# Attention on one core: query products in the scores' third PSUM bank, and the upper value products in tiles 4, 5, 8, 9 instead of 8 to 11

## The chip, the core and the metric

The kernel runs on one core of a Trainium2 chip. The metric is the device time of one execution in microseconds (us), lower is better. The core has four compute engines that each run their own instruction stream in order and meet at semaphores: TensorE (PE, matrix products), VectorE (DVE), ScalarE (ACT) and GpSimd (POOL); SyncE (SP) issues the DMAs. PE writes its products into PSUM, which has 8 banks of 128 partitions by 512 float32; DVE and ACT read it.

## The reference

Two batches of 1024 tokens with 128 channels pass a small mixture attention (called ffn), a causal attention with 16 heads and one shared key/value head, and the mixture attention again. The changed part is the causal attention:

```
q   = (x @ Wq).reshape(b, n, 16, 64).transpose(0, 2, 1, 3) * 64 ** -0.5
kv  = concatenate([null_kv, x @ Wkv], axis=1)          # 1 + 1024 rows of 64
sim = where(causal_mask, -max, einsum('bhid,bjd->bhij', q, kv))
out = einsum('bhij,bjd->bhid', softmax(sim), kv)       # keys and values are the same rows
x   = x + out.reshape(b, n, 1024) @ Wout
```

## The kernel before

The two ffn phases and the attention follow one another. The attention works on pairs of heads: 8 pairs in each of the two batches, 16 pairs numbered by `pg`. A pair is 16 tiles (`STEPS`), called tiles 0 to 15 below: 2 query halves (qh) x 2 heads (hh) x 4 query blocks of 128. Tile t has `n = 1 + 128 * (qt + 1)` key columns, so tiles 0 to 3 and 4 to 7 have 129 to 513 columns and tiles 8 to 11 and 12 to 15 have 641 to 1025. All engines follow the same list of tiles, written out by hand; pairs 2 to 5 of each batch run in a hardware loop, the others are written out. For each tile

- PE computes the scores of tile t (`a_score_tile`, L1276), once `a_exp` says that the exponentials of tile t-2 are done; then transposes the normalized probabilities of tile t-4 (`a_transposes`, L1289), in up to two groups, even groups through bank 5, odd groups through bank 6;
- DVE takes the row maximum of tile t (`a_maximum`, L992), copies the even group of tile t-4 out of PSUM (`a_evac`, L1011), and computes the reciprocal of the row sum of tile t-2 and the null key's probability (`a_recip`, L1000, L1002);
- ACT copies the odd group of tile t-4 (`a_evac`, L695) and takes the exponentials of tile t (`a_exps`, L685);
- POOL normalizes tile t (`normalize`, L578).

Between these, some tiles carry extra work. PE multiplies the previous pair's probabilities with the values: lower query half (qh 0) after tiles 0 and 1 (`V0_STEPS`), upper half (qh 1) in four parts after tiles 8, 9, 10, 11 (`V1_STEPS`); both by `a_values`, L1305. DVE moves each finished half out of PSUM (`o_evac`, L1016), one tile later. PE also projects the next pair's queries, one token half after tile 3 and one after tile 6 (`queries`, L1256). ACT takes the first bf16 part of that product (`q_first`, L667), DVE the rest (`q_rests`, L985), ACT the second part (`q_second`, L672), POOL the third (`q_third`), and SP copies the parts into `q_s`, from which the next pair's tile 0 reads. At the first pair of batch 1 (pg = 8) PE also transposes the null probabilities (L1315) and projects batch 0's output (L1323) after tiles 12, 13 and 14.

Even tiles write their scores from bank 3 on, odd tiles from bank 0 on. A tile of 1025 columns (11 and 15, both odd) needs a third bank, bank 2, for its last column. Bank 7 (`PV_BANK`) holds in turn: lower values, query half 0, query half 1, upper values. So each of these four waits until DVE has emptied the bank of the one before (`pv_bank_free`).

Of the kernel before, what the change touches and what calls it, by code (L numbers as in the profile page):

```python
# [7 lines left out]
ALU = mybir.AluOpType  # L8
# [8 lines left out]
def build(nc, x_in, a_wq, a_wkv, a_null, a_wout, f_wq, f_bq, f_wk, f_bk, f_wv, f_bv,  # L17
          f_wg1, f_bg1, f_wg2, f_bg2, f_wo, f_bo, out):
    B, T, _ = x_in.shape
# [20 lines left out]
    with ExitStack() as ctx:  # L40
# [122 lines left out]
        GATE_BANK = [6, 1]  # L163
        Y_BANK = [0, 1, 5, 6]
        T_BANK = [5, 6]

        w_loaded = sem("w_loaded")
        wo_loaded = sem("wo_loaded")
# [9 lines left out]
        k3_ready = sem("k3_ready")  # L178
        keys_ready = sem("keys_ready")
        proj_done = sem("proj_done")  # L180
        q1_ready = sem("q1_ready")
        q2_ready = sem("q2_ready")
        q3_ready = sem("q3_ready")
# [75 lines left out]

        V0_STEPS = (0, 1)  # L260
        Q_STEPS = (3, 6)
        V1_STEPS = (8, 9, 10, 11)
        P0_STEPS = (12, 13)
        Y_STEPS = (13, 14)

        def q_uses(pg, first, h):

            return (2 if first else 4 * pg + 1) + h

        N_USES = sum(len(v) for v in USES)  # L270

# [330 lines left out]
        def _(act):  # L602
# [59 lines left out]
            def q_first(pg, par, h):  # L662

                if h == 0 and (not isinstance(pg, int) or pg >= 1):
                    act.wait_ge(q_s_loaded[1 - par], 48 * (pg - 1 - (1 - par)) + 96)
                act.wait_ge(proj_done, 2 * pg + h + 1)
                nc.scalar.activation(q_part[:, 0, h * HALF:(h + 1) * HALF], ps[:, PV_BANK, :], ACT.Copy,  # L667
                                     scale=A_SCALE).then_inc(q1_ready, 1)

            def q_second(pg, h, k):  # L670
                act.wait_ge(pv_bank_free, k + 1)
                nc.scalar.activation(q_part[:, 1, h * HALF:(h + 1) * HALF], q_rest[:, h * HALF:(h + 1) * HALF],  # L672
                                     ACT.Copy).then_inc(q2_ready, 1)

# [29 lines left out]
            def attention():  # L704
                norm_std(B, 0)
                norm_T(B, 0, 5)
                q_first(0, 0, 0)
                values_out(0)
                key_part(0, 0)
                q_second(0, 0, 0)  # L710
                q_first(0, 0, 1)
                key_part(0, 1)
                q_second(0, 1, 1)
                key_part(0, 2)
                for b in range(1, B):
                    norm_std(B + b, b)
                    norm_T(B + b, b, 5)
                    values_out(b)
                    for k in range(3):
                        key_part(b, k)  # L720
                act.wait_ge(null_done, 1)
                nc.scalar.activation(null_out[:, :], ps[0:AH, 5, 0:C], ACT.Copy).then_inc(null_ready, 1)  # L722

                def body(b, pl, switch, first, last):
                    for k in range(2):
                        pg = b * PAIRS + pl + k
                        turn = switch and k == 0
                        for t in range(NS):
                            if turn and t - 1 in P0_STEPS:
                                p0_evac(b - 1, P0_STEPS.index(t - 1), PV_BANK)  # L730
                            if t >= A_LAG:
                                a_evac(pg, t - A_LAG)
                            elif not (first and k == 0):
                                a_evac(pg - 1, NS + t - A_LAG)
                            if t - 1 in Q_STEPS and not (last and k == 1):
                                q_first(pg + 1, (k + 1) % 2, Q_STEPS.index(t - 1))
                            a_exps(pg, t)
                            if t - 1 in Q_STEPS and not (last and k == 1):
                                h = Q_STEPS.index(t - 1)
                                q_second(pg + 1, h, q_uses(pg, first and k == 0, h))  # L740
# [12 lines left out]
                hidden(B)  # L753
                gate_exp(B)
                split(B)
# [53 lines left out]
        def _(dve):  # L809
# [169 lines left out]
            def q_rests(pg, h):  # L979

                if h == 0 and (not isinstance(pg, int) or pg >= 1):
                    dve.wait_ge(q3_ready, 2 * pg)
                dve.wait_ge(q1_ready, 2 * pg + h + 1)
                s = slice(h * HALF, (h + 1) * HALF)
                nc.vector.scalar_tensor_tensor(q_rest[:, s], ps[:, PV_BANK, :], A_SCALE, q_part[:, 0, s], ALU.mult,  # L985
                                               ALU.subtract).then_inc(pv_bank_free, 1)

            def a_maximum(pg, t):

# [124 lines left out]
        def _(pe):  # L1114
# [132 lines left out]
                                           start=True, stop=True)  # L1247
                ins.then_inc(av_done, 1)

            def queries(pg, k, b, par, h):  # L1250

                if h == 0:
                    pe.wait_ge(wq_loaded[par], 8 * (pg - par) + 16)
                if not isinstance(pg, int) or k > 0:
                    pe.wait_ge(pv_bank_free, k)
                nc.tensor.matmul(ps[:, PV_BANK, :], wq_pair[:, par, :], xnT[:, b, h * HALF:(h + 1) * HALF],  # L1256
                                 start=True, stop=True).then_inc(proj_done, 1)

            def a_score_tile(pg, b, par, t):

                qh, hh, qt = STEPS[t]
                n = 1 + (qt + 1) * P
                if t == 0:
                    pe.wait_ge(q_s_loaded[par], 48 * (pg - par) + 96)
                if t >= 2 or not isinstance(pg, int) or pg >= 1:
                    pe.wait_ge(a_exp, NS * pg + t - 1)
                cols = slice(qt * P, (qt + 1) * P)
                for c0 in range(0, n, HALF):
                    c1 = min(n, c0 + HALF)
                    m0, m1 = max(c0, 1 + qt * P), c1  # L1270
                    bank = S_BANK[t % 2] + c0 // HALF
# [55 lines left out]
            def attention():  # L1327
# [13 lines left out]
                def body(b, pl, switch, first, last):  # L1341
                    for k in range(2):
# [3 lines left out]
                        bn = b + 1 if isinstance(pl, int) and pl + k == PAIRS - 1 else b  # L1346
                        no_q = last and k == 1
                        for t in range(NS):
                            a_score_tile(pg, b, k, t)
# [4 lines left out]
                            if t in V0_STEPS and not (first and k == 0):  # L1354
                                if switch and k == 1 and t == V0_STEPS[0]:
                                    pe.wait_ge(x_ready, 2 * B + 2 * b)
                                a_values(pg - 1, bb, 0, 4 * pg, V0_STEPS.index(t))
                            if t in Q_STEPS and not no_q:
                                h = Q_STEPS.index(t)
                                queries(pg + 1, q_uses(pg, first and k == 0, h), bn, (k + 1) % 2, h)  # L1360
                            if t in V1_STEPS and not (first and k == 0):
                                a_values(pg - 1, bb, 1, 4 * pg + (1 if no_q else 3), V1_STEPS.index(t))
                            if turn and t in P0_STEPS:
                                h = P0_STEPS.index(t)
                                if h == 0:
                                    pe.wait_ge(pv_bank_free, 4 * pg + 4)
# [14 lines left out]
                    body(b, PAIRS - 2, False, False, b == B - 1)  # L1381
                pg = B * PAIRS - 1
                for part in range(2):
                    a_values(pg, B - 1, 0, 4 * pg + 2, part)
                for t in range(NS - A_LAG, NS):
                    a_transposes(pg, t)
                for part in range(4):
                    a_values(pg, B - 1, 1, 4 * pg + 3, part)

                norm_T(2 * B, 0, 5)  # L1390
                pe.wait_ge(a_exp, NS * (pg + 1))
# [4 lines left out]
                pe.wait_ge(pv_bank_free, 4 * (pg + 1))  # L1396
                outputs(B - 1, 0, 0)
                project(B, 0)
                outputs(B - 1, 1, 1)
# [1 line left out]
            def ffn(ph):  # L1401
# [24 lines left out]
                if ph == 0:  # L1426

                    norm_T(B, 0, 5)
                    pe.wait_ge(xnT_ready, 2 * B + 2)
                    queries(0, 0, 0, 0, 0)  # L1430
                    keys(0)
                finish_1(ph)
                if ph == 0:
                    queries(0, 1, 0, 0, 1)
                finish_last(ph)

            ffn(0)
# [25 lines left out]
```

## Time and profile before

| | |
|---|---|
| time, median of 3 runs | 1442.69 us (1442.65 to 1443.37) |
| the profiled execution | 1439.09 us |
| its span, first to last instruction | 1437.3 us, so 1.8 us lie around it |
| mean granted TensorE clock | 0.958 of 2.4 GHz |
| busy: PE, DVE, ACT, POOL | 1259.6, 1120.4, 931.9, 332.8 us |

The attention's pairs lie between 431 us and about 1021 us of the span. The profile gives, for each instruction or run of like instructions, its start, its duration, and in square brackets how long the engine had stood still before it and which instruction released it. Durations of neighbouring matrix products overlap, so what a piece of PE's work takes is read from start to start. A row of the view of busy times holds: the stretch, its length, busy us (and instructions) of PE, PE's weight loads, DVE, ACT and POOL, the granted TensorE clock (1.00 is 2.4 GHz, 0.50 is 1.2 GHz), the busy share of the DMA engines, and GB/s.

### The profile page before, as it was taken

What the parts mean: (1) busy time and instruction counts of PE and PEld (TensorE: products, weight loads), DVE (VectorE), ACT (ScalarE), POOL (GpSimd) and SP (SyncE); (2) the same over time, 40 slices, a digit from 0 to 9 for tenths busy, and PEclk for the clock granted to TensorE, in tenths of its full rate; (3) what the DMA queues carried; (4) which work ended last, traced back from release to release, by engine and by line L of the source; (5) the groups of instructions that cost most, each with busy time, mean ns of one, the idle gap of its engine ahead of it and who ended that gap; (6) DMA issues with size and microseconds to landing.
All of it is one profiled execution on the core that took longest, in us unless ns stands there. A gap on an engine that the chain in (4) does not pass through costs nothing. (4 is left out here: it accounts for less than half of the span.)

```text
span 1437.3 us, 32130 instructions
## 1 busy us (share of the span) xinstructions
PE 1259.6 (88%) x10416; PEld 549.8 (38%) x10416; DVE 1120.4 (78%) x1941; ACT 931.9 (65%) x1915; POOL 332.8 (23%) x552
## 2 busy tenths in 40 slices
PE   3699999999759999999988999999867999999996
PEld 2122222222235555555556555555552222222222
DVE  6899999999857666666634666666648999999997
ACT  3288899889736555555533555555422999898894
POOL 4300000010004333334422333343322000000200
PEclk9599999999979999999999999999986999999998
DMA  4612213542122222222220222222042221235422
GB/s 118 184 44 61 59 49 74 85 82 64 42 44 47 47 47 47 46 46 47 47 47 1 47 47 46 46 47 45 1 132 89 54 57 53 60 81 86 81 54 59
DMA packets 58915, 86.59 MB, mean 60 GB/s; under 512 B 22288, under 2 KB 32464, under 8 KB 58832
## 3 DMA queue, kind: packets, MB, share of 16 engines
q1 hardware_dynamic: 58832, 85.53, 25.7%
q8 instruction: 46, 0.75, 0.2%
q14 instruction: 37, 0.30, 0.1%
HBM read 37.79 MB, written 22.54 MB: 42 GB/s over the span
## 5 line engine op out<-in xcount | busy, mean ns | idle before, releaser
L916 DVE TENSOR_REDUCE neg_max<-ps 128x1 f32<-128x1024 f32 x512 | 589.5, 1211 | 36.8 <-PE ps L1157 35.5
L771 ACT ACTIVATE arena<-ps 128x512 f32<-128x512 f32 x1024 | 551.3, 595 | 101.0 <-PE ps L1172 85.3
L1188 PE MATMUL ps<-arena 128*32 128x256 f32 x4096 | 328.9, 393 | 34.7 <-ACT arena L761 33.1
L1172 PE MATMUL ps<-arena 50*128 50x512 bf16 x1024 | 323.5, 387 | 6.9 <-DMA arena<-max_dram 6.7
L992 DVE TENSOR_REDUCE a_neg_max<-ps 128x1 f32<-128x129 f32 (+7 forms) x256 | 193.2, 755 | 168.5 <-PE ps L1276 165.0
L1157 PE MATMUL ps<-arena 48*128 48x512 bf16 x1024 | 305.8, 397 | 18.5 <-DVE neg_max L916 16.5
L578 POOL TENSOR_SCALAR arena<-arena,a_rsum 128x128 f32<-128x128 f32 (+7 forms) x256 | 191.4, 748 | 376.1 <-DVE a_rsum L1000 365.0
L1276 PE MATMUL ps<-arena 128*128 128x512 bf16 (+4 forms) x1344 | 239.7, 305 | 9.6 <-ACT null_out L722 4.9
L685 ACT ACTIVATE arena<-ps,a_neg_max 128x129 f32<-128x129 f32 (+7 forms) x256 | 189.5, 741 | 60.7 <-DVE a_neg_max L992 58.5
L695 ACT ACTIVATE arena<-ps 128x128 f32<-128x128 f32 (+1 forms) x192 | 87.0, 453 | 206.6 <-PE ps L1289 205.3
L1289 PE MATMUL ps<-ident,arena 128*128 128x128 f32 x1152 | 174.6, 279 | 20.7 <-DVE arena L1011 20.5
L1276 PEld LDWEIGHTS ps<-arena 128*128 128x128 bf16 x1344 | 109.7, 98 | 153.2 <-ACT arena L685 47.9
L1188 PEld LDWEIGHTS ps<-arena 128*32 128x32 f32 x4096 | 81.3, 108 | 225.3 <-issue 118.9
L1172 PEld LDWEIGHTS ps<-arena 50*128 50x128 bf16 x1024 | 71.6, 93 | 248.7 <-ACT arena L771 230.2
L1305 PE MATMUL ps<-arena 128*64 128x512 f32 (+3 forms) x768 | 144.1, 498 | 12.9 <-DVE arena L985 12.1
L1289 PEld LDWEIGHTS ps<-ident,arena 128*128 128x128 f32 x1152 | 122.7, 140 | 37.3 <-DVE arena L1011 15.1
L498 POOL CAST max_parts<-neg_max 128x8 bf16<-128x8 f32 x64 | 12.1, 189 | 495.5 <-DVE neg_max L916 495.5
L1011 DVE COPY arena<-ps 128x512 f32<-128x512 f32 (+1 forms) x192 | 113.9, 593 | 4.9 <-PE ps L1289 3.8
L1305 PEld LDWEIGHTS ps<-arena 128*64 128x64 f32 x768 | 47.9, 136 | 70.8 <-issue 56.7
L1157 PEld LDWEIGHTS ps<-arena 48*128 48x128 bf16 x1024 | 54.6, 94 | 35.7 <-DVE neg_max L916 30.1
L1002 DVE TENSOR_TENSOR p<-arena,a_rsum 128x1 f32<-128x1 f32 (+1 forms) x256 | 49.4, 193 | 22.9 <-DVE a_rsum L1000 1.4
L1276 PE MATMUL ps<-causal,ident_bf 128*128 128x128 bf16 (+2 forms) x320 | 61.2, 208 | 0.0
(120 smaller groups left out, 801.6 us busy)
## 6 DMA issues: line engine op xcount, KB each, us to landing
arena<-stack_dram SPq DMA_DIRECT2D x128, 192.0 KB, 3.4
stack_dram<-arena SPq DMA_DIRECT2D x48, 256.0 KB, 3.9
arena<-arena SPq DMA_DIRECT2D x32, 384.0 KB, 4.4
o_dram<-arena SPq DMA_DIRECT2D x32, 256.0 KB, 2.1
arena<-arena SPq DMA_DIRECT2D x32, 256.0 KB, 5.0
arena<-o_dram SPq DMA_DIRECT2D x30, 256.0 KB, 4.5
arena<-max_dram SPq DMA_DIRECT2D x256, 1.0 KB
arena<-arena SPq DMA_DIRECT2D x32, 128.0 KB, 4.8
```

Source lines behind the costliest of these rows:

```text
L578: nc.gpsimd.tensor_scalar(a_probs[:, t % RING, 1:n], a_probs[:, t % RING, 1:n], a_rsum[:, t:t + 1], 1.0, ALU.mult, ALU.mult).then_inc(a_no ...
L685: nc.scalar.activation(a_probs[:, t % RING, 0:n], ps[:, S_BANK[t % 2]:S_BANK[t % 2] + (n + HALF - 1) // HALF, :].rearrange("p a b -> p (a ...
L771: nc.scalar.activation(probs[:, t, :], ps[:, EXP_BANK[t], :], ACT.Exp, scale=F_SCALE).then_inc(probs_ready, 1)
L916: nc.vector.tensor_reduce(neg_max[:, g, t:t + 1], ps[:, bank:bank + 2, :].rearrange("p a b -> p (a b)"), AX, ALU.max, negate=True).then_in ...
L992: nc.vector.tensor_reduce(a_neg_max[:, t:t + 1], ps[:, S_BANK[t % 2]:S_BANK[t % 2] + (n + HALF - 1) // HALF, :].rearrange("p a b -> p (a b ...
L1011: nc.vector.tensor_copy(probs_T[qh][:, hh, kt:kt + m, (qt % 4) * P:(qt % 4 + 1) * P], ps[:, T_BANK[0], 0:m * P].rearrange("p (k q) -> p k ...
L1157: ins = nc.tensor.matmul(ps[:, bank + h, :], stack[rows, g, 0, t * P:(t + 1) * P], stack[rows, g, 1, h * HALF:(h + 1) * HALF], start=True, ...
L1172: ins = nc.tensor.matmul(ps[:, bank, :], stack[rows, g, 1, kt * P:(kt + 1) * P], stack[rows, g, 0, h * HALF:(h + 1) * HALF], start=True, s ...
L1188: ins = nc.tensor.matmul(ps[row:row + 32, PV_BANK, cols], v_unit[:, g, t // 2, :], probs[:, t, cols], start=j == 0 and half == 0 and g % 2 ...
L1276: ins = nc.tensor.matmul(ps[:, bank, o0:o1], lhs, rhs, start=k == 0, stop=k == len(passes) - 1)
L1289: ins = nc.tensor.transpose(ps[:, T_BANK[use % 2], j * P:(j + 1) * P], a_probs[:, t % RING, 1 + (kt + j) * P:1 + (kt + j + 1) * P], ident[ ...
L1305: ins = nc.tensor.matmul(ps[hh * AD:(hh + 1) * AD, PV_BANK, q0:HALF], av[:, b, kt, :], probs_T[qh][:, hh, kt, q0:HALF], start=kt == 0, sto ...
```

## The change

Query products of all pairs but the first go to bank 2 (`Q_BANK`), which has a semaphore of its own, `q_bank_free`. Query half 0 no longer waits for a bank, half 1 waits for DVE's `q_rests` of half 0, and a score tile of 1025 columns (in practice tile 11) waits until both halves have been read. The value bank alternates between lower and upper values only. The four parts of the upper value products stand after tiles 4, 5, 8, 9, and with the last of them `o_evac` moves on DVE from the slot of tile 12 to that of tile 10.

```diff
+        Q_BANK = 2
...
+        q_bank_free = sem("q_bank_free")
...
-        V1_STEPS = (8, 9, 10, 11)
+        V1_STEPS = (4, 5, 8, 9)
...
-            def q_second(pg, h, k):
-                act.wait_ge(pv_bank_free, k + 1)
+            def q_second(pg, h):
+                if isinstance(pg, int) and pg == 0:
+                    act.wait_ge(pv_bank_free, h + 1)
+                else:
+                    act.wait_ge(q_bank_free, 2 * pg + h - 1)
...
-                nc.vector.scalar_tensor_tensor(q_rest[:, s], ps[:, PV_BANK, :], A_SCALE, q_part[:, 0, s], ALU.mult,
-                                               ALU.subtract).then_inc(pv_bank_free, 1)
+                initial = isinstance(pg, int) and pg == 0
+                nc.vector.scalar_tensor_tensor(q_rest[:, s], ps[:, PV_BANK if initial else Q_BANK, :], A_SCALE, q_part[:, 0, s],
+                                               ALU.mult, ALU.subtract).then_inc(pv_bank_free if initial else q_bank_free, 1)
...
-                if not isinstance(pg, int) or k > 0:
-                    pe.wait_ge(pv_bank_free, k)
-                nc.tensor.matmul(ps[:, PV_BANK, :], wq_pair[:, par, :], xnT[:, b, h * HALF:(h + 1) * HALF],
+                else:
+                    pe.wait_ge(pv_bank_free if initial else q_bank_free, 1 if initial else 2 * pg - 1)
+                nc.tensor.matmul(ps[:, PV_BANK if initial else Q_BANK, :], wq_pair[:, par, :], xnT[:, b, h * HALF:(h + 1) * HALF],
...
+                if n > 2 * HALF and not no_q:
+                    pe.wait_ge(q_bank_free, 2 * pg + 2)
...
-                                a_values(pg - 1, bb, 0, 4 * pg, V0_STEPS.index(t))
+                                a_values(pg - 1, bb, 0, 2 * pg, V0_STEPS.index(t))
...
-                                a_values(pg - 1, bb, 1, 4 * pg + (1 if no_q else 3), V1_STEPS.index(t))
+                                a_values(pg - 1, bb, 1, 2 * pg + 1, V1_STEPS.index(t))
```

The other edits renumber the waits on `pv_bank_free` to match.

PE in the loop of pairs, before, from the first query product (after tile 3) on. L1276 are scores (three passes and the causal one), L1289 transposes:

```order
859 L1256 MATMUL ps<-xnT,wq_pair 128x512
860 L1276 MATMUL ps<-arena 128x129 x3
861 L1276 MATMUL ps<-causal,ident_bf 128x128
862 L1289 MATMUL ps<-ident,arena 128x128
863 L1276 MATMUL ps<-arena 128x257 x3
864 L1276 MATMUL ps<-causal,ident_bf 128x128
865 L1289 MATMUL ps<-ident,arena 128x128 x2
866 L1276 MATMUL ps<-arena 128x385 x3
867 L1276 MATMUL ps<-causal,ident_bf 128x128
868 L1289 MATMUL ps<-ident,arena 128x128 x3
869 L1256 MATMUL ps<-xnT,wq_pair 128x512
```

The same stretch of the changed kernel, whose line numbers have moved (L1260 query product, L1282 scores, L1295 transposes, L1311 values):

```order
858 L1260 MATMUL ps<-xnT,wq_pair 128x512
859 L1282 MATMUL ps<-arena 128x129 x3
860 L1282 MATMUL ps<-causal,ident_bf 128x128
861 L1295 MATMUL ps<-ident,arena 128x128
862 L1311 MATMUL ps<-arena 64x512 x4
863 L1282 MATMUL ps<-arena 128x257 x3
864 L1282 MATMUL ps<-causal,ident_bf 128x128
865 L1295 MATMUL ps<-ident,arena 128x128 x2
866 L1311 MATMUL ps<-arena 64x512 x4
867 L1282 MATMUL ps<-arena 128x385 x3
868 L1282 MATMUL ps<-causal,ident_bf 128x128
869 L1295 MATMUL ps<-ident,arena 128x128 x3
```

Two value parts of four products each now stand behind the transposes of tiles 4 and 5, ahead of the second query product. Behind tile 8 stood before the first of these full-width parts; tiles 10 and 11 carried the last two.

DVE in the same loop, before, from the slot of tile 10 (maximum L992, copy L1011, reciprocal L1000, null probability L1002) into that of tile 12:

```order
899 L992 TENSOR_REDUCE a_neg_max<-ps 128x1
900 L1010 REGISTER_ALU
901 L1011 COPY arena<-ps 128x4x128
902 L1000 RECIPROCAL a_rsum<-a_sum 128x1
903 L1002 ISA
904 L1002 TENSOR_TENSOR p<-arena,a_rsum 128x1
905 L1015 REGISTER_ALU
906 L1016 ISA
907 L1016 TENSOR_SCALAR arena<-ps 128x512
908 L991 REGISTER_ALU
```

These rows are the slot of tile 12, with `o_evac` (L1016) at its end. In the changed kernel it ends the slot of tile 10, whose copy is three blocks wide:

```order
888 L1013 REGISTER_ALU
889 L1014 COPY arena<-ps 128x3x128
890 L1003 RECIPROCAL a_rsum<-a_sum 128x1
891 L1005 ISA
892 L1005 TENSOR_TENSOR p<-arena,a_rsum 128x1
893 L1018 REGISTER_ALU
894 L1019 ISA
895 L1019 TENSOR_SCALAR arena<-ps 128x512
896 L994 REGISTER_ALU
897 L995 TENSOR_REDUCE a_neg_max<-ps 128x1
```

The move of bank 7 from PSUM now stands between the null probability of tile 8 and the maximum of tile 11.

## Rows read from the trace of the kernel before

**Rows 1.** Busy time by engine: one pair, and two parts of it.

```profile
566.22:602.22 36.00, 33.77 (x229) 19.00 (x228) 25.18 (x65) 19.94 (x49) 14.27 (x19) 1.00 0.21 46
584.00:592.00 8.00, 8.00 (x51) 3.52 (x49) 4.05 (x9) 3.07 (x6) 1.55 (x3) 1.00 0.83 181
595.00:600.00 5.00, 4.48 (x35) 2.98 (x34) 4.59 (x10) 2.85 (x6) 2.53 (x3) 1.00 0.00 0
```

**Rows 2.** PE's waits, 440 to 1010 us: total us, times, longest.

```profile
PE ps L1289 <- DVE arena L1011: 18.2, 29, 0.8
PE ps L1305 <- DVE arena L985: 12.1, 14, 1.0
```

**Rows 3.** Timeline of PE in one pair: start us, us, instruction, [idle before].

```profile
576.29 1.02 PE L1256 MATMUL ps<-xnT,wq_pair 128*128 128x512 f32 x2
577.46 0.82 PE L1276 MATMUL ps<-arena 128*128 128x512 bf16 x3
...
580.82 1.94 PE L1305 MATMUL ps<-arena 128*64 128x512 f32 x8 [0.81 <-DVE arena L985]
...
583.73 0.39 PE L1289 MATMUL ps<-ident,arena 128*128 128x128 f32 x2
584.05 1.94 PE L1305 MATMUL ps<-arena 128*64 128x512 f32 x8
585.92 1.31 PE L1276 MATMUL ps<-arena 128*128 128x512 bf16 x6
...
587.55 1.72 PE L1305 MATMUL ps<-arena 128*64 128x512 f32 x8
589.21 1.47 PE L1276 MATMUL ps<-arena 128*128 128x512 bf16 x6
...
591.24 0.87 PE L1305 MATMUL ps<-arena 128*64 128x256 f32 x8
592.04 0.99 PE L1276 MATMUL ps<-arena 128*128 128x512 bf16 x6
...
593.48 1.14 PE L1276 MATMUL ps<-arena 128*128 128x512 bf16 x6
...
597.20 0.98 PE L1289 MATMUL ps<-ident,arena 128*128 128x128 f32 x7 [0.52 <-DVE arena L1011]
...
601.53 0.76 PE L1289 MATMUL ps<-ident,arena 128*128 128x128 f32 x5 [0.75 <-DVE arena L1011]
```

**Rows 4.** Timeline of DVE in the same pair.

```profile
580.07 0.69 DVE L985 SCALAR_TENSOR_TENSOR arena<-ps,arena 128x512 f32<-128x512 f32 x1 [0.26 <-ACT arena L667]
...
587.33 1.09 DVE L992 TENSOR_REDUCE a_neg_max<-ps 128x1 f32<-128x897 f32 x1 [2.06 <-PE ps L1276]
...
589.10 0.16 DVE L1002 TENSOR_TENSOR p<-arena,a_rsum 128x1 f32 x1
...
594.76 0.16 DVE L1002 TENSOR_TENSOR p<-arena,a_rsum 128x1 f32 x1
594.99 0.69 DVE L1016 TENSOR_SCALAR arena<-ps 128x512 f32 x1
595.60 0.95 DVE L992 TENSOR_REDUCE a_neg_max<-ps 128x1 f32<-128x769 f32 x1
```

**Rows 5.** Timeline of DVE in the first pair: the maximum of tile 11.

```profile
448.29 1.22 DVE L992 TENSOR_REDUCE a_neg_max<-ps 128x1 f32<-128x1025 f32 x1
```

**Rows 6.** Timeline of PE in the first pair: tile 13, and the next pair's first transposes.

```profile
450.80 1.15 PE L1276 MATMUL ps<-arena 128*128 128x512 bf16 x6 [0.37 <-ACT arena L685]
...
458.14 0.63 PE L1289 MATMUL ps<-ident,arena 128*128 128x128 f32 x4 [0.85 <-DVE arena L1011]
```

**Rows 7.** Timeline of PE in the pair with batch 0's output.

```profile
738.63 0.60 PE L1315 MATMUL ps<-ident,p 128*16 128x128 f32 x4 [1.83 <-DVE arena L1016]
...
756.42 3.07 PE L1323 MATMUL ps<-wout,arena 128*128 128x128 f32 x16 [1.88 <-DVE x L1023]
```

**Rows 8.** Busy time by engine behind the last of these; columns as in rows 1.

```profile
757.20:764.20 7.00, 7.00 (x32) 6.33 (x30) 0.00 (x0) 0.00 (x0) 0.00 (x0) 0.51 0.00 0
```

More of the change, by code:

```diff
@@ L261, in build @@
         Q_STEPS = (3, 6)
-        V1_STEPS = (8, 9, 10, 11)
+        V1_STEPS = (4, 5, 8, 9)
         P0_STEPS = (12, 13)
         Y_STEPS = (13, 14)
-        def q_uses(pg, first, h):
-            return (2 if first else 4 * pg + 1) + h
         N_USES = sum(len(v) for v in USES)
@@ L666, in q_first @@
                 act.wait_ge(proj_done, 2 * pg + h + 1)
-                nc.scalar.activation(q_part[:, 0, h * HALF:(h + 1) * HALF], ps[:, PV_BANK, :], ACT.Copy,
+                bank = PV_BANK if isinstance(pg, int) and pg == 0 else Q_BANK
+                nc.scalar.activation(q_part[:, 0, h * HALF:(h + 1) * HALF], ps[:, bank, :], ACT.Copy,
                                      scale=A_SCALE).then_inc(q1_ready, 1)
-            def q_second(pg, h, k):
-                act.wait_ge(pv_bank_free, k + 1)
+            def q_second(pg, h):
[3 more added lines that the diff above has]
+                    act.wait_ge(q_bank_free, 2 * pg + h - 1)
                 nc.scalar.activation(q_part[:, 1, h * HALF:(h + 1) * HALF], q_rest[:, h * HALF:(h + 1) * HALF],
@@ L709, in attention @@
                 key_part(0, 0)
-                q_second(0, 0, 0)
+                q_second(0, 0)
                 q_first(0, 0, 1)
                 key_part(0, 1)
-                q_second(0, 1, 1)
+                q_second(0, 1)
                 key_part(0, 2)
@@ L739, in body @@
                                 h = Q_STEPS.index(t - 1)
-                                q_second(pg + 1, h, q_uses(pg, first and k == 0, h))
+                                q_second(pg + 1, h)
                 for b in range(B):
@@ L1248, in keys, with queries, a_score_tile @@
                 ins.then_inc(av_done, 1)
-            def queries(pg, k, b, par, h):
+            def queries(pg, b, par, h):
+                initial = isinstance(pg, int) and pg == 0
                 if h == 0:
                     pe.wait_ge(wq_loaded[par], 8 * (pg - par) + 16)
-                if not isinstance(pg, int) or k > 0:
-                    pe.wait_ge(pv_bank_free, k)
-                nc.tensor.matmul(ps[:, PV_BANK, :], wq_pair[:, par, :], xnT[:, b, h * HALF:(h + 1) * HALF],
+                else:
+                    pe.wait_ge(pv_bank_free if initial else q_bank_free, 1 if initial else 2 * pg - 1)
+                nc.tensor.matmul(ps[:, PV_BANK if initial else Q_BANK, :], wq_pair[:, par, :], xnT[:, b, h * HALF:(h + 1) * HALF],
                                  start=True, stop=True).then_inc(proj_done, 1)
-            def a_score_tile(pg, b, par, t):
+            def a_score_tile(pg, b, par, t, no_q):
                 qh, hh, qt = STEPS[t]
@@ L1348, in body @@
                         for t in range(NS):
-                            a_score_tile(pg, b, k, t)
+                            a_score_tile(pg, b, k, t, no_q)
                             if t >= A_LAG:
@@ L1356, in body @@
                                     pe.wait_ge(x_ready, 2 * B + 2 * b)
-                                a_values(pg - 1, bb, 0, 4 * pg, V0_STEPS.index(t))
+                                a_values(pg - 1, bb, 0, 2 * pg, V0_STEPS.index(t))
                             if t in Q_STEPS and not no_q:
                                 h = Q_STEPS.index(t)
-                                queries(pg + 1, q_uses(pg, first and k == 0, h), bn, (k + 1) % 2, h)
+                                queries(pg + 1, bn, (k + 1) % 2, h)
                             if t in V1_STEPS and not (first and k == 0):
-                                a_values(pg - 1, bb, 1, 4 * pg + (1 if no_q else 3), V1_STEPS.index(t))
+                                a_values(pg - 1, bb, 1, 2 * pg + 1, V1_STEPS.index(t))
                             if turn and t in P0_STEPS:
@@ L1365, in body @@
                                 if h == 0:
-                                    pe.wait_ge(pv_bank_free, 4 * pg + 4)
+                                    pe.wait_ge(pv_bank_free, 2 * pg + 2)
                                 else:
@@ L1383, in attention @@
                 for part in range(2):
-                    a_values(pg, B - 1, 0, 4 * pg + 2, part)
+                    a_values(pg, B - 1, 0, 2 * pg + 2, part)
                 for t in range(NS - A_LAG, NS):
@@ L1387, in attention @@
                 for part in range(4):
-                    a_values(pg, B - 1, 1, 4 * pg + 3, part)
+                    a_values(pg, B - 1, 1, 2 * pg + 3, part)
                 norm_T(2 * B, 0, 5)
@@ L1395, in attention @@
                 pe.wait_ge(p0T_ready, 2 * B)
-                pe.wait_ge(pv_bank_free, 4 * (pg + 1))
+                pe.wait_ge(pv_bank_free, 2 * (pg + 2))
                 outputs(B - 1, 0, 0)
@@ L1429, in ffn @@
                     pe.wait_ge(xnT_ready, 2 * B + 2)
-                    queries(0, 0, 0, 0, 0)
+                    queries(0, 0, 0, 0)
                     keys(0)
@@ L1433, in ffn @@
                 if ph == 0:
-                    queries(0, 1, 0, 0, 1)
+                    queries(0, 0, 0, 1)
                 finish_last(ph)
```

## The prediction

> **What bounds the kernel now.** I read the busy times over one pair first. Of 36.0 us PE is busy 33.8, DVE 25.2, ACT 19.9, POOL 14.3, at the full clock [rows 1]. So PE bounds the attention; the change gives it neither more nor less work, and what it can win is some of the 2.2 us per pair in which PE stands still. The view of waits says for whom: 29 waits for DVE's copies of transposed probabilities, 18.2 us in all, and 14 waits of the value products for DVE's `q_rests`, 12.1 us, longest 1.0 [rows 2]. The 14 are pairs 1 to 14; the last pair has no next queries and pair 0 no earlier values.
>
> PE's timeline shows where these lie. After tile 8 the upper values stand still 0.81 us (end of the wait 580.82): bank 7 holds query half 1, which DVE reads from 580.07 on, when ACT's first part is out [rows 3, 4]. After tile 14 PE waits 0.52 us and after the next tile 0 again 0.75 us, for DVE's copies; and tile 7 starts 0.15 us past the end of the query product, a short wait for an exponential [rows 3]. The first wait is what the new bank removes. The second and third come from DVE being late in tiles 12 to 15, where PE has no value products to do. That is the point of the forecast: with parts 3 and 4 gone from tiles 10 and 11, this stretch without cover grows from four tiles to six.
>
> **The change, part by part.** I work on the looped pair of rows 3 and 4, call "0" the end of tile 9's scores, 583.73, and treat the tiles before and behind it apart.
>
> *Tiles 4 to 9, gain.* Query half 0 gets its bank at once; before, it did not stand still either. Upper part 1 after tile 4 needs the previous pair's last copies, but tile 4's own transposes need the same DVE copy already, so no new wait: I take 0 (bounds: 0, and 0.7 us per pair, the length of one such DVE instruction, if the copy were a whole slot late). The removed wait of 0.81 us counts fully, since values no longer follow `q_rests`. The 0.15 us before tile 7 goes too, because tiles 4 and 5 now carry 1.87 us of values each (584.05 to 585.92) [rows 3] and ACT has that much longer. About 0.1 to 0.2 us more is in the quick tiles 4 and 5, each of which follows an exponential closely. Gain 1.1 to 1.2 us.
>
> *Tile 10 to the next pair's tile 0, loss.* Before, from 583.73 to the transposes at 601.53 is 17.8 us [rows 3]. In it stand value parts of 1.87 us (584.05 to 585.92) and 1.66 us (587.55 to 589.21) that now lie before "0": like for like 17.8 - 3.53 = 14.27 us. Now the same stretch after the change, in us after "0":
> - PE: transposes 0.32, then the short last part 0.80 (591.24 to 592.04), so tile 10's scores start at 1.12. Its maximum started 1.41 after its scores did (585.92, 587.33), so now at 2.53. Tile 10's scores and transposes take 1.63 (585.92 to 587.55), tile 11's 2.03 (589.21 to 591.24), tile 12's 1.44 (592.04 to 593.48): PE reaches tile 11 at 2.75, tile 12 at 4.78, and could start tile 13 at 6.22 [rows 3, 4].
> - DVE: from tile 10's maximum to its null probability 1.77 (587.33 to 589.10), then `o_evac`, 0.23 to its start and 0.61 to the next instruction (594.76, 594.99, 595.60) [rows 4]. So tile 11's maximum starts at 2.53 + 2.61 = 5.14, though its scores are done by about 4.4. Without `o_evac` there it would be 4.4 to 4.5.
> - ACT and PE: tile 13 needs the exponentials of tile 11. In the first pair, which has no values and waits for exactly this (0.37 us, released by ACT), tile 13 starts 2.51 after tile 11's maximum (448.29, 450.80) [rows 5, 6]. So now 5.14 + 2.51 = 7.65: a **new wait of about 1.4 us**. Queued behind it on PE are the transposes of tiles 9 to 12 and all that follows.
> - From tile 13's start to the next pair's first transposes the first pair took 7.34 us (450.80 to 458.14), with the same last wait (0.85) [rows 6] and with DVE no later than it would be here. So the transposes come at 14.99.
>
> The loss is 14.99 - 14.27 = 0.7 us. The 0.52 us wait after tile 14 is inside the 14.27 and vanishes: DVE has caught up during PE's stall. The 0.75 us wait stays, since it hangs on tile 15's maximum and the copy behind it.
>
> *Sum of a pair.* 1.1 to 1.2 gained, 0.7 lost: 0.5 us less of 36.0. 13 ordinary pairs (1 to 7, 9 to 14) give 6.5 us. The pairs written out differ from the looped ones by 0.1 us in both terms.
>
> *Pair 8*, with batch 0's output, has the same gain of 1.1 at tile 8, and a second one: its null transposes waited 1.83 us for `o_evac` (738.63) [rows 7], which now stands two tiles earlier. Tile 13's exponential wait takes part of that back. By the same walk tile 13 starts some 1.2 us earlier against like work, instead of 0.7 later: 1.1 + 1.2, about 2.4 us with the rest. *Pair 15* has no wait to win after tile 8 and pays the loss: -0.5. *Pair 0* has no upper values and stays.
>
> *What costs nothing.* The query product of half 1 comes 3.5 us later (two parts of 1.87 ahead, less the short wait), and so do ACT's and DVE's parts, GpSimd's third part and the DMAs into `q_s`. They were at work up to about 593 in the old order (DMA share 0.83 from 584 to 592, 0.00 from 595 to 600), and the next tile 0 needs them at about 600 [rows 1]: end at 596.5 against 599.8, 3 us of cover. If it were gone, each us late would cost one. Tile 11's wait for `q_bank_free` is met 4 us before: DVE's read ends at 580.76 + 3.5 = 584.3 in the old order's times, tile 11 starts 2.75 behind "0", which then lies at about 586.2. Reading bank 2 for tile 15 ends before tile 3 of the next pair, which already waits for tile 1's exponentials.
>
> **Total.** 6.5 + 2.4 - 0.5 = 8.4 us, from 1439.1 of the profiled execution to 1430.7. The timed runs' median is 3.6 us above that execution; I subtract from the median: **1434.3 us**, -0.6%. A measurement of this kernel can tell about 0.2% (2.9 us) from no change.
>
> **The rivals.**
>
> *A. The stall at tile 13 eats the gain.* Each 0.1 us that DVE or ACT is later than walked in tiles 10 to 12 adds 0.1 us to all 15 pairs. Between no late `o_evac` (tile 11's maximum at 4.4: loss of nearly 0) and a slot longer by one more 512-wide DVE move (0.61: loss 1.3) the attention gains 17 us or loses about 1. For the long end speaks that DVE, ACT and PE hand over at every tile there; against it that pair 0 ran the same six tiles with nothing but these dependences, and its time is in my sum. Net within 0.2%: 1440 to 1445.
>
> *B. The clock falls in the stall: slower.* The only fall of the granted clock within the pairs' stretch comes behind a PE wait of 1.88 us (756.42) [rows 7]; the clock was 0.51 for the next 7.0 us [rows 8], which costs half, 3.5 us. The wait of 1.83 us (738.63) had no such fall behind it. The new stall of 1.4 us comes 14 times, close behind the busiest stretch, with 0.75 following 7 us later. If every third stall brought a fall, 5 x 3.5 = 17.5 us against 8.4 gained: 1452. It decides from the third fall on. Against it: it is shorter than both. The Trainium skill ("TensorE: Matmul & The Clock Gate", "A second HAM failure mode: psum-queue depth-cycling") describes a kernel whose many short stops between groups of products made the clock swing between its two levels; by it, this change would come out as in B. The trace before has three such stops in the pair of rows 3 and shows 1.00 over it [rows 1], so I give that little weight.
>
> *C. The clock does not fall at pair 8.* PE's waits there get shorter. If the fall behind 756.42 goes, 3.5 us more are won: 1431.
>
> *D. The removed wait only moves.* If the values after tile 4 wait for the last copies as long as those after tile 8 did for `q_rests`, the gain of 1.1 goes and the loss of 0.7 stays: 15 x 0.7 less 2 for pair 8, slower by 8: 1451. In the last pair nothing stands between, and there PE does wait for that copy; in the others the query product, 1.02 us long [rows 3], covers it.
>
> **How the numbers follow.** Forecast 1434 (1430 to 1438) 0.58; C 0.12; A 0.18, of which 0.04 still faster than 0.2%; B 0.05; D 0.07. Range 1429.5 to 1440.5: it leaves out most of A's far side, B and D. Faster by over 0.2%: 0.74; (0.58 + 0.12 + 0.04); within: 0.14; slower: 0.12 (B and D).
>
> **What the changed profile should show.** The waits for `q_rests` by value products gone (12.1 us). In each pair a wait of 1.2 to 1.4 us at tile 13's scores, released by ACT's exponentials; no wait at the transposes after tile 14; the one of 0.75 to 0.85 us behind tile 0 as before; a pair in 35.5 us. In pair 8 the null transposes don't wait for `o_evac`. PE's busy time unchanged. The forecast is wrong if the stall at tile 13 exceeds 2 us, if values after tile 4 stand still, if tile 11 waits for `q_bank_free`, if tile 0 waits for a DMA, or if the granted clock leaves 1.00 within pairs 1 to 15 other than once.

## The result and the profile after

The changed kernel takes 1427.0 us (median of 4 runs, 1423.6 to 1429.1) against 1442.7 us before; the ratio is 0.9891, 95% interval [0.9873, 0.9909]. It is faster by 15.6 us. The forecast was 8.4 us, and 1427.0 lies below the range, which began at 1429.5. The direction and each wait that was named came as forecast; the size that was forecast is about half of the measured one.

The profiled execution of the changed kernel took 1426.65 us, with a span of 1424.9. The view of PE's waits between 440 and 1010 us (total us, times, longest) answers to [rows 2]:

```profile
PE ps L1282 <- ACT arena L687: 17.8, 18, 1.2
PE ps L1295 <- DVE arena L1014: 12.7, 16, 0.8
```

The wait of the value products for `q_rests` is gone. In its place stand waits of score tiles for ACT's exponentials, 17.8 us, longest 1.2; the waits of transposes for DVE's copies are down from 29 to 16. Apart from these the view has only two waits of pair 8's output products (1.9 and 1.4 us) and 0.3 us without a releaser: tile 11 does not wait for `q_bank_free`, and tile 0 does not wait for a DMA. PE's busy time, forecast unchanged, reads 1248.4 us for 1259.6, but over 10352 records for 10416, so this says little.

PE's timeline of one pair in the loop of the changed kernel, which answers to [rows 3]:

```profile
575.19 0.33 PE L1295 MATMUL ps<-ident,arena 128*128 128x128 f32 x1
575.48 1.94 PE L1311 MATMUL ps<-arena 128*64 128x512 f32 x8
...
579.93 0.66 PE L1282 MATMUL ps<-arena 128*128 128x385 bf16 x3
...
582.97 0.98 PE L1282 MATMUL ps<-arena 128*128 128x512 bf16 x6
...
584.05 1.72 PE L1311 MATMUL ps<-arena 128*64 128x512 f32 x8
...
586.75 0.39 PE L1295 MATMUL ps<-ident,arena 128*128 128x128 f32 x2
...
594.39 1.15 PE L1282 MATMUL ps<-arena 128*128 128x512 bf16 x6 [1.23 <-ACT arena L687]
...
597.29 0.94 PE L1295 MATMUL ps<-ident,arena 128*128 128x128 f32 x7
...
601.57 0.77 PE L1295 MATMUL ps<-ident,arena 128*128 128x128 f32 x5 [0.75 <-DVE arena L1014]
```

The values after tile 4 (575.48) follow the transposes without standing still. Tile 13 (594.39) waits 1.23 us for ACT, as in all eight looped pairs; in the written-out ones this wait is 0.96 or 0.97 us, and 0.53 in pair 8. The transposes after tile 14 (597.29) have no wait; the last one, 0.75, is unchanged. The next two fences, of DVE and of ACT in the same pair, show the chain that makes the new wait:

```profile
591.04 0.16 DVE L1005 TENSOR_TENSOR p<-arena,a_rsum 128x1 f32 x1
591.27 0.69 DVE L1019 TENSOR_SCALAR arena<-ps 128x512 f32 x1
591.88 1.22 DVE L995 TENSOR_REDUCE a_neg_max<-ps 128x1 f32<-128x1025 f32 x1
```

```profile
588.74 0.19 ACT L687 ACTIVATION_READ_ACCUMULATOR arena<-ps,a_neg_max 128x1 f32 x1
590.40 1.01 ACT L687 ACTIVATE arena<-ps,a_neg_max 128x897 f32<-128x897 f32 x1 [1.47 <-DVE a_neg_max L995]
...
593.13 1.12 ACT L687 ACTIVATE arena<-ps,a_neg_max 128x1025 f32<-128x1025 f32 x1 [1.00 <-DVE a_neg_max L995]
```

`o_evac` (591.27) stands ahead of tile 11's maximum (591.88); ACT stands still until that is done (593.13), and PE's tile 13 until ACT is (594.39).

To compare kernels apart from what happens outside the pairs, the table takes the distance between the transposes that open pair 1 and pair 15 (the row of 601.53 in [rows 3] is one of these), and within it pair 8 by itself. "Saved per pair" is over the other 13 pairs, 465.99 us before. The ratios of times are each to the kernel before, run beside it on the same chip. Each distance is from one profiled execution; pair 8 is longer where the clock fell in it (before, changed, bank alone again, copy first).

| kernel | 13 pairs, us | saved per pair | pair 8 | time against the kernel before |
|---|---|---|---|---|
| before | 465.99 | | 64.11 | |
| changed | 453.32 | 0.97 | 59.42 | 0.989 [0.987, 0.991] |
| changed, another chip | 453.33 | 0.97 | 59.39 | 0.988 [0.985, 0.990] |
| bank alone | 454.37 | 0.89 | 59.95 | 0.992 [0.990, 0.995] |
| bank alone, again | 454.49 | 0.88 | 64.68 | 0.991 [0.988, 0.993] |
| `o_evac` in tile 12's slot | 446.93 | 1.47 | 59.13 | 0.982 [0.979, 0.985] |
| values 4, 5, 10, 11 | 462.52 | 0.27 | 60.37 | 0.995 [0.992, 0.997] |
| one more DVE instruction | 461.36 | 0.36 | 58.44 | 0.994 [0.991, 0.996] |
| `o_evac` on ACT | 444.95 | 1.62 | 57.26 | 0.981 [0.978, 0.983] |
| the same, copy first in tile 15 | 438.03 | 2.15 | 58.28 | 0.975 [0.973, 0.978] |
| bank alone, `q_second` later | 454.39 | 0.89 | 59.94 | 0.992 [0.989, 0.994] |

Where a program was profiled twice (changed, bank alone), the two executions agree within 0.12 us over 13 pairs, so this distance tells far more than the times do.

### The profile page after: what moved, and what is told of

Its sections match the earlier page's. It is cut to its first block and busy times, and to the rows that moved or that the text cites. A ratio compares the mean times of both kernels' runs of the same rounds, so it can differ in the third digit from the quotient of the medians.

```text
span 1424.9 us, 32069 instructions
## 1 busy us (share of the span) xinstructions
PE 1248.4 (88%) x10352; PEld 549.4 (39%) x10416; DVE 1116.7 (78%) x1941; ACT 930.8 (65%) x1915; POOL 332.6 (23%) x552
## 5 line engine op out<-in xcount | busy, mean ns | idle before, releaser
L1282 PE MATMUL ps<-arena 128*128 128x512 bf16 (+4 forms) x1280 | 225.6, 301 | 27.6 <-ACT arena L687 18.1
L1295 PE MATMUL ps<-ident,arena 128*128 128x128 f32 x1152 | 172.3, 277 | 14.9 <-DVE arena L1014 14.6
L1282 PEld LDWEIGHTS ps<-arena 128*128 128x128 bf16 x1344 | 110.8, 98 | 165.7 <-issue 59.9
L1311 PE MATMUL ps<-arena 128*64 128x512 f32 (+3 forms) x768 | 144.2, 498 | 0.8 <-DVE arena L1014 0.7
L1295 PEld LDWEIGHTS ps<-ident,arena 128*128 128x128 f32 x1152 | 122.8, 140 | 25.4 <-DVE arena L1014 8.8
L1311 PEld LDWEIGHTS ps<-arena 128*64 128x64 f32 x768 | 47.5, 136 | 57.7 <-issue 47.9
L1282 PE MATMUL ps<-causal,ident_bf 128*128 128x128 bf16 (+2 forms) x320 | 61.1, 208 | 0.0
L1005 DVE TENSOR_TENSOR p<-arena,a_rsum 128x1 f32<-128x1 f32 (+1 forms) x256 | 42.8, 167 | 22.9 <-DVE a_rsum L1003 1.5
```

Of the source, the lines that this page charges most:

```text
L1295: ins = nc.tensor.transpose(ps[:, T_BANK[use % 2], j * P:(j + 1) * P], a_probs[:, t % RING, 1 + (kt + j) * P:1 + (kt + j + 1) * P], ident[ ...
L1311: ins = nc.tensor.matmul(ps[hh * AD:(hh + 1) * AD, PV_BANK, q0:HALF], av[:, b, kt, :], probs_T[qh][:, hh, kt, q0:HALF], start=kt == 0, sto ...
```

## The experiments

**The bank alone.**

```diff
-        V1_STEPS = (4, 5, 8, 9)
+        V1_STEPS = (8, 9, 10, 11)
```

> Query products in bank 2, all four upper value parts back after tiles 8 to 11. Theory M (my walk, corrected by the changed kernel's trace): the whole gain per pair is 1.5 us won in tiles 4 to 9 less 0.55 us lost from tile 10 on; the bank brings 1.0 of it (the wait after tile 8, 0.81 shown, 0.99 from start to start), the moved values bring 0.5 and cost 0.55, so they are worth about nothing. Then the bank alone gives 14 x 1.0 us and the time is about that of the changed kernel, 1427 to 1430; a pair takes 35.0 us, the 0.52 us wait after tile 14 stays, tile 13 does not wait for ACT. Rival N: the gain comes from the value products moved into the light tiles, and a pair with the bank alone only moves its wait to tile 10 to 14 where DVE is late: less than 0.3 us per pair, time 1438 or more.

Measured 1430.1 us, ratio 0.992. PE's timeline of a looped pair:

```profile
575.03 0.66 PE L1282 MATMUL ps<-arena 128*128 128x385 bf16 x3
...
578.51 0.98 PE L1282 MATMUL ps<-arena 128*128 128x512 bf16 x6
...
579.75 1.94 PE L1311 MATMUL ps<-arena 128*64 128x512 f32 x8
...
596.13 0.98 PE L1295 MATMUL ps<-ident,arena 128*128 128x128 f32 x7 [0.52 <-DVE arena L1014]
...
600.46 0.77 PE L1295 MATMUL ps<-ident,arena 128*128 128x128 f32 x5 [0.76 <-DVE arena L1014]
```

The values after tile 8 follow its scores in 1.24 us (578.51 to 579.75); before it was 2.07 (578.75 to 580.82). The late waits stay as they were and do not grow. So the bank alone saves 0.89 us of the 0.97 per pair (M had 1.0), and the moved values add 0.08. Theory M holds; the rival that the moved values bring the gain has fallen. Run again beside the changed kernel on one chip:

> The bank alone again, on the same chip as the changed kernel, to settle how the gain divides. Theory M: its pairs in the loop take 35.18 us against 35.0, so 2 to 3 us slower in the pairs, and 3 us slower at the pair with batch 0's output, where the null transposes keep their wait of 1.83 us: 4 to 6 us slower than the changed kernel. Rival N: with 11 us of 15.6 as first measured the difference is only the spread between chips, and both are equal within 1 us.

> The changed kernel again, on the chip of the two above, to compare them with. Ratio to the kernel before 0.989 as measured at first, pairs of 35.0 us; the medians may lie apart by some us in the stages outside the pairs, since the granted clock falls at places that differ from run to run.

Measured 1432.0 and 1428.0 us, 3.9 apart. M had 4 to 6. In the 13 pairs the difference is 1.2 us, where M had 2 to 3, and in pair 8, with the cost of the falling clock taken out of both (below), 2.1 us, where M had 3. The six runs of each kernel range over 7 and 12 us, so the 3.9 us of the medians is no finer test than that.

**`o_evac` back in tile 12's slot.**

```diff
-                            if t - 1 == V1_STEPS[-1] and not (first and k == 0):
+                            if t == 12 and not (first and k == 0):
                                 o_evac(pg - 1, before[1], 1)
```

> The changed kernel, with DVE's move of the upper values (o_evac) back in the slot of tile 12 instead of tile 10. Theory M: that instruction (0.61 us and 0.23 us of lead) delays tile 11's maximum, and through the exponentials tile 13: the wait at tile 13 falls from 1.23 us to 0.3 to 0.5 us, but DVE is then later at tiles 13 and 14, so PE waits 0.2 to 0.3 us again after tile 14: net 0.4 us per pair, 15 x 0.4 = 6 us less than the changed kernel, about 1421. Rival N: the wait at tile 13 is set by ACT's and PE's own hand-overs, not by DVE's extra work, and stays above 1 us; time as the changed kernel's within 1 us.

Measured 1417.3 us, ratio 0.982. PE in a looped pair:

```profile
595.16 1.15 PE L1282 MATMUL ps<-arena 128*128 128x512 bf16 x6 [0.53 <-ACT arena L687]
...
598.00 0.22 PE L1282 MATMUL ps<-causal,ident_bf 128*128 128x128 bf16 x1
598.25 0.98 PE L1295 MATMUL ps<-ident,arena 128*128 128x128 f32 x7
...
602.58 0.66 PE L1295 MATMUL ps<-ident,arena 128*128 128x128 f32 x4 [0.76 <-DVE arena L1014]
```

Tile 13's wait falls from 1.23 to 0.53 us, and from tile 13 to the last wait PE takes 7.42 us, against 7.18 in the changed kernel: the work that moved back costs 0.24 us there. Most of it stands between tile 14 and its transposes: 0.25 us (598.00 to 598.25) for 0.06 in the changed kernel, a wait like the one M named, though the idle column shows none. Saved 0.49 per pair more, M's figure was 0.4. The rival's 1 us wait did not come.

**One more DVE instruction in tile 10's slot.**

```diff
                 dve.wait_ge(apv_done, 2 * pg + qh + 1)
+                if qh:
+                    nc.vector.tensor_reduce(extra[:, bass.ds(pl, 1)], ps[:, PV_BANK, :], AX, ALU.max)
```

> The changed kernel with one more DVE instruction in tile 10's slot, a maximum over the 512 columns of the value bank that nobody uses (0.60 us, up to 0.23 us of lead in the loop). Theory M: DVE is on the chain there, so tile 11's maximum and tile 13's scores come 0.6 to 0.85 us later in each of 15 pairs: the wait at tile 13 is 1.9 us in place of 1.23, and the time 9 to 12 us more, 1436 to 1439. Rival N: DVE has slack there (it is 78% busy over the kernel), nothing changes, 1427.

Measured 1433.6 us, ratio 0.994. DVE, then PE, in a looped pair:

```profile
595.61 0.69 DVE L1021 TENSOR_REDUCE extra<-ps 128x512 f32 x1
596.22 0.68 DVE L1022 TENSOR_SCALAR arena<-ps 128x512 f32 x1
596.82 1.22 DVE L996 TENSOR_REDUCE a_neg_max<-ps 128x1 f32<-128x1025 f32 x1
```

```profile
599.33 1.15 PE L1285 MATMUL ps<-arena 128*128 128x512 bf16 x6 [1.83 <-ACT arena L688]
```

The instruction takes 0.61 us (595.61 to 596.22) and tile 13's wait goes from 1.23 to 1.83: one for one. The pairs lose 0.62 each. The whole kernel's time is a little under M's 1436; its five runs lie between 1431.6 and 1439.5 us, so the difference is not clear of their spread. DVE is on the chain in this slot, though before the change it was idle for 11 of 36 us in a pair [rows 1].

**Values 4, 5, 10, 11.**

```diff
-        V1_STEPS = (4, 5, 8, 9)
+        V1_STEPS = (4, 5, 10, 11)
```

> The changed kernel with the last two upper value parts after tiles 10 and 11 instead of 8 and 9 (so o_evac is in tile 12's slot). Theory M: the parts in tiles 10 and 11 cover DVE's lateness. Walk: from tile 9's scores to the next pair's transposes as before the change, 15.9 us with part 3 inside, against 14.8 + 1.66 = 16.5 in the changed kernel: 0.55 us less per pair, tiles 4 to 9 keep their gain. No wait at tile 13, the 0.5 us wait after tile 14 back. Time about 1419, 8 us under the changed kernel. Rival N: what matters is only how much value work lies in tiles 4 to 9; with less of it there the gain shrinks and the time is 1427 or more.

Measured 1433.7 us: a pair takes 0.71 us more than in the changed kernel, where M had 0.55 less. This is a miss. PE and ACT in a looped pair:

```profile
583.66 1.15 PE L1282 MATMUL ps<-arena 128*128 128x512 bf16 x6 [0.86 <-ACT arena L687]
...
585.37 1.31 PE L1282 MATMUL ps<-arena 128*128 128x512 bf16 x6 [0.27 <-ACT arena L687]
...
596.64 0.98 PE L1295 MATMUL ps<-ident,arena 128*128 128x128 f32 x7 [0.52 <-DVE arena L1014]
```

```profile
582.35 0.59 ACT L666 ACTIVATE arena<-ps 128x512 bf16<-128x512 f32 x1
582.82 0.69 ACT L687 ACTIVATE arena<-ps,a_neg_max 128x513 f32<-128x513 f32 x1
583.39 0.21 ACT L687 ACTIVATION_READ_ACCUMULATOR arena<-ps,a_neg_max 128x1 f32 x1
```

Tile 13's wait is gone as M said, but tile 9 now waits 0.86 us and tile 10 0.27 us. Tile 9 needs tile 7's exponentials (582.82), and ACT takes query half 1's first part (582.35) ahead of them. In the changed kernel the 1.66 us of values after tile 8 cover this; I moved them and did not ask what they covered. The rival's number (1427 or more) came true. Its reason, that only the amount of value work in tiles 4 to 9 counts, does not hold: the bank alone has the same two parts in these tiles, after 8 and 9, and saves 0.89 us per pair where this kernel saves 0.27. What counts is which wait a part stands in front of.

**`o_evac` on ACT, ahead of tile 10's exponentials.**

```diff
+            def o_evac_1(pg, pl):
+                act.wait_ge(apv_done, 2 * pg + 2)
+                nc.scalar.activation(o_T[:, bass.ds(pl, 1), HALF:2 * HALF].rearrange("p a b -> p (a b)"),
+                                     ps[:, PV_BANK, :], ACT.Copy).then_inc(pv_bank_free, 1)
...
+                            if t - 1 == V1_STEPS[-1] and not (first and k == 0):
+                                o_evac_1(pg - 1, PAIRS - 1 if turn else pl + k - 1)
```

> The changed kernel with the upper values moved out of PSUM by ACT in tile 10's slot, ahead of its exponentials, instead of by DVE. In the changed kernel's trace ACT stands still 1.47 us just there. Theory M (DVE's slot of tile 10 delays tile 11's maximum and through it tile 13): DVE loses 0.84 us of work in the dense tiles and ACT does it for nothing: the wait at tile 13 falls from 1.23 to about 0.5 us, and unlike with o_evac in tile 12's slot nothing comes back later (7.2 us from tile 13 to the next transposes, not 7.4). A pair takes 34.3 us: 10 us less than the changed kernel, 3 to 4 less than with o_evac at tile 12; ratio to the kernel before 0.980 to 0.984. Rival N: ACT is on the same chain (its exponentials of tile 10 gate tile 12), so the work only changes engine; at most 2 us less than the changed kernel.

Measured 1415.7 us, ratio 0.981 [0.978, 0.983], 12.3 us under the changed kernel on the same chip. ACT, then PE, in a looped pair:

```profile
585.80 0.59 ACT L702 ACTIVATE arena<-ps 128x512 f32 x1
587.36 1.01 ACT L687 ACTIVATE arena<-ps,a_neg_max 128x897 f32<-128x897 f32 x1 [0.98 <-DVE a_neg_max L1002]
```

```profile
590.64 1.15 PE L1287 MATMUL ps<-arena 128*128 128x512 bf16 x6 [0.52 <-ACT arena L687]
```

ACT takes the values out in 0.59 us and still stands still 0.98 us before tile 10's exponentials, where it stood 1.47: the work is in its idle time. Tile 13 waits 0.52 us, as M said. The pairs save 0.64 us each over the changed kernel, where M had 0.7; over `o_evac` in tile 12's slot it is 2.0 us in 13 pairs, less than the 3 to 4 that M had.

**The same, and DVE's copy first in tile 15's slot.**

```diff
+                            if t == 15:
+                                a_evac(pg, t - A_LAG)
                             a_maximum(pg, t)
-                            if t >= A_LAG:
+                            if t == 15:
+                                pass
+                            elif t >= A_LAG:
                                 a_evac(pg, t - A_LAG)
```

> As the kernel with o_evac on ACT, and in tile 15's slot DVE copies the probabilities of tile 11 before it takes tile 15's maximum. Theory M: the wait of 0.75 us behind the next tile 0 (in every trace so far) hangs on the maximum of 1.14 us that stands ahead of this copy; with the copy first, PE waits about 0.1 us, tile 15's exponentials come 1.05 us later, and tile 1 then waits 0.1 to 0.3 us for them: 0.4 to 0.6 us less per pair, a pair of 33.8 to 33.9 us, 6 to 9 us less than without the swap. Rival N: the later maximum delays tile 1 and everything behind it as much as it frees tile 0: no change or slower.

Measured 1407.9 us, ratio 0.975 [0.973, 0.978], 7.8 us less again. PE around the next tile 0, and DVE:

```profile
596.99 0.33 PE L1291 MATMUL ps<-arena 128*128 128x129 bf16 x3
...
597.50 0.77 PE L1304 MATMUL ps<-ident,arena 128*128 128x128 f32 x5
```

```profile
596.76 0.69 DVE L1021 COPY arena<-ps 128x512 f32<-128x512 f32 x1 [0.62 <-PE ps L1304]
597.36 1.22 DVE L1002 TENSOR_REDUCE a_neg_max<-ps 128x1 f32<-128x1025 f32 x1
```

The copy now ends ahead of the maximum and the transposes follow tile 0 in 0.51 us instead of 1.15. Without pairs 8 and 9 a pair is shorter by 0.62 us on average, so the later maximum costs nothing that shows there; in pair 9 it delays batch 0's last output, for which values now wait 1.2 us, and the pair is 0.5 us longer instead. This is the fastest version of the study, 20 us under the changed kernel on the same chip.

**`q_second` one tile later, on the bank alone.**

```diff
-                            if t - 1 in Q_STEPS and not (last and k == 1):
-                                h = Q_STEPS.index(t - 1)
+                            if t - 2 in Q_STEPS and not (last and k == 1):
+                                h = Q_STEPS.index(t - 2)
                                 q_second(pg + 1, h)
```

> The bank alone, with ACT's second query part (q_second) one tile later in ACT's order, behind the exponentials of tiles 5 and 8 instead of ahead of them. It asks what the short waits of tiles 6 and 7 are, which I undervalued: from tile 6's scores to tile 8's PE took 3.48 us before and with the bank alone, 3.04 us with values ahead of it, and the idle column shows almost none of it. Theory M: PE waits there for tile 5's exponentials, which stand behind q_second on ACT, and q_second waits 0.83 us for DVE's q_rests. With q_second later the stretch takes 3.05 us without any value product moved, and a pair in the loop 34.7 to 34.8 us instead of 35.18. Rival N: the difference is issue overhead of PE around the query product or a slower handling of back-to-back small tiles; then the stretch stays at 3.48 us and the pair at 35.2 us.

Measured 1428.6 us; the pairs are the same as with the bank alone. PE in a looped pair:

```profile
575.32 0.66 PE L1282 MATMUL ps<-arena 128*128 128x385 bf16 x3
...
578.49 0.98 PE L1282 MATMUL ps<-arena 128*128 128x512 bf16 x6
...
579.74 0.33 PE L1295 MATMUL ps<-ident,arena 128*128 128x128 f32 x1 [0.21 <-POOL arena L576]
580.05 1.94 PE L1311 MATMUL ps<-arena 128*64 128x512 f32 x8
```

Tile 6 to tile 8 takes 3.17 us instead of 3.48, where M had 3.05: 0.31 us of it was the wait for tile 5's exponentials behind `q_second`. But tile 8 to its values takes 1.56 us instead of 1.24: tile 4's transposes now wait for GpSimd. The 0.31 us is given back at once. M's pair of 34.7 to 34.8 us was wrong.

## Why the forecast had the right sign and the wrong size

*The wait after tile 8 goes, values after tile 4 do not wait.* Right: rival D did not come.

*"Gain 1.1 to 1.2 us" in tiles 4 to 9.* This is the step that failed: the term was mis-sized. Over 13 pairs it makes some 5 of the 8.7 us by which the pairs saved more than forecast. Measured, with the moved values taken out: from the transposes that open the pair (565.53, the like of 601.53) to 583.73 PE took 18.20 us before; now from 566.57 to 586.75 it is 20.18, less 3.53 us of moved values 16.65. The gain is 1.55 us. The removed wait is worth 0.99 from tile 8's scores to its values (2.07 to 1.08 us), not the 0.81 that stands in brackets. From tile 6's scores to tile 8's PE took

```profile
575.27 0.66 PE L1276 MATMUL ps<-arena 128*128 128x385 bf16 x3
...
578.75 0.98 PE L1276 MATMUL ps<-arena 128*128 128x512 bf16 x6
```

3.48 us before (the two rows above), and takes 3.04 in the changed kernel: 0.44, where I had 0.15 for tile 7's wait and 0.1 to 0.2 for all the rest. Of the last 0.12 us nothing is left between the pair's first transposes and tile 4 (8.38 to 8.21), since from tile 4 to its own transposes PE takes as much more (0.23 to 0.41); it lies in tile 5, which takes 0.71 us without its values for 0.83. The run with `q_second` later shows 0.31 of the 0.44 to be the wait for tile 5's exponentials; that the rest is GpSimd's normalization was not tried apart.

*The walk from tile 10 on, loss 0.7.* Every step of it came: tile 13 at 7.65 behind "0" was 7.64 (586.75 to 594.39), tile 11's maximum at 5.14 was 5.13 and tile 13 again followed it by 2.51, the wait of "about 1.4" shows as 1.23, the one after tile 14 vanished. The forecast gave every pair this wait of 1.2 to 1.4 us; the written-out pairs have 0.97. There `o_evac` starts 0.07 us after the start of the instruction ahead of it, in the looped ones 0.23, and the walk had taken the looped figure. From tile 13 to the last wait it is 7.18 us and not 7.34; I had taken this from pair 0, which is written out, and written-out pairs also show 0.85 for the last wait where looped ones show 0.75. The loss is 14.82 - 14.27 = 0.55 us.

*Sum of a pair.* 1.55 - 0.55 = 1.0 in the loop, 0.97 over the 13 pairs, where I had 0.5: 12.7 us for 6.5. *Pair 15* lost 0.2 us (32.40 to 32.62 us from its first transposes to the values behind them), not 0.5. *Pair 8* saved 4.7 us for 2.4: PE there shows

```profile
733.14 1.15 PE L1282 MATMUL ps<-arena 128*128 128x512 bf16 x6 [0.53 <-ACT arena L687]
...
750.50 3.52 PE L1329 MATMUL ps<-wout,arena 128*128 128x128 f32 x16 [1.88 <-DVE x L1026]
```

The null transposes no longer wait, tile 13 waits 0.53 us. The product of 750.50 takes 3.52 us, but the next ones 2.05: the clock fell as before the change [rows 8], for a shorter time. That fall cost 3.2 us before and 1.6 now (from the wait's end through the second output half 12.7 and 11.2 us, against 9.6 in the runs where it did not fall), so 1.6 of the 4.7 is the clock, which the sum had at nothing, and 3.1 the waits, for 2.4. The 3.5 us that rivals B and C set for this fall is 3.2 so measured.

*Total.* The pairs save 12.7 + 4.7 - 0.2, with all digits 17.1 us, between these two executions (562.5 and 545.4 us from pair 1's transposes to pair 15's end). The spans differ by 12.4, because the changed kernel's execution lost 4 us ahead of the attention; the medians differ by 15.6.

*Rival A* was right in its price, 0.1 us for 0.1 us, which the extra instruction shows, and the stall stayed as short as walked. *Rival B*: in the changed kernel and in all experiments the granted clock was 1.00 over pairs 1 to 7 and 9 to 14, with stalls at tile 13 of 1.83 us in each of the eight looped pairs of the kernel with the extra instruction. The Trainium skill's account in "TensorE: Matmul & The Clock Gate", "A second HAM failure mode: psum-queue depth-cycling" does not describe this kernel: none of these stops brought a fall. *Rival C*: the fall at pair 8 comes in some executions and not in others, of kernels with the same wait of 1.88 us, so neither it nor its shorter length can be put down to the change. The rival's case, that it goes, did not come in the two profiled executions of the changed kernel.

## What to carry to other kernels

When one buffer is shared by two chains, count which other order the sharing forces: here one more bank gave nine tenths of the gain of an ordinary pair (12.3 of the 16.2 us of the medians on one chip), and moving the products gave almost none, until the DVE instruction that followed them was put back two tiles later (0.49 us per pair) or on an engine that stood idle at that place (0.64). Before moving work out of a tile, ask what it covers there: the same 1.66 us of products hid a 0.86 us wait after tile 8 and their move made it visible. Read a removed wait from start to start, against a pair where it is absent, not from its idle time.

## What the runs showed of the hardware

- Idle time in PE's rows understates waits. Records of neighbouring products overlap by 0.1 to 0.2 us, so a wait of that length shows no idle time at all (tile 6 to tile 8: 0.44 us won, 0.15 to be seen), and a shown wait of 0.81 was worth 0.99.
- Single executions of one program swing by more than the 0.2% (2.9 us) that I had called tellable: on one chip the kernel before took 1439.7 to 1448.0 us in 11 runs. For medians 0.2% was near: the intervals of the ratios reach 0.2 to 0.3% to either side. The changed kernel's two profiled executions took 1426.65 and 1433.7 us, but from pair 1 to pair 15 both take 512.7 us, so this swing comes from outside the pairs. One source is the granted clock ahead of the attention, in the busy times of the changed kernel below; in its other execution the same stretch stood at 0.86, and in the kernel before at 1.00.

```profile
150.00:200.00 50.00, 46.88 (x456) 11.49 (x456) 43.63 (x43) 41.50 (x79) 2.73 (x13) 0.90 0.18 50
```

- Behind the wait of about 1.88 us in pair 8, which every kernel has, the granted clock fell in 5 of 11 profiled executions (the first one to three output products behind it took 2.7 to 3.8 us each) and stayed at full in the other 6 (2.05 us each). The changed kernel fell both times, the bank alone once of two. Stops of 1.83 us at tile 13 brought no fall in eight pairs. What decides it is open.
